# The middle stage's attention: probabilities turned unnormalised, four output products scaled by VectorE

## The reference

```python
q = rope(rmsnorm(x @ Wq.T, q_norm_w))        # 32 heads of 128
k, v = x @ Wk.T, x @ Wv.T                    # 8 heads of 128
# keys and values: 512 rows of a paged cache (gathered by a block table), then the 128 new ones
scores = q @ keys.T / sqrt(128) + mask       # 640 keys for each query
probs  = softmax(scores)                     # rows sum to 1
ctx    = probs @ values
out    = ctx.reshape(128, 32 * 128) @ Wo.T   # a sum over the 32 heads
```

## Time and profile before

| | |
|---|---|
| time, median of 3 runs | 1362.9 us (1361.45 to 1364.13) |
| span of the profiled execution | 1360.4 us |
| busy TensorE (matmul) | 1317.0 us, 97% |
| busy VectorE | 1077.3 us, 79% |
| busy ScalarE | 862.2 us, 63% |
| busy GpSimd | 653.2 us, 48% |

### The profile page before, as it was taken

One profiled execution on the slowest core, in us unless ns is written; L12 is line 12 of the kernel. 1 busy time (PEld: TensorE's weight loads), 2 busy tenths in 40 slices (PEclk: granted clock), 3 DMA queues, 4 the chain that ended last, 5 costly groups with the idle time before them and its releaser, 6 DMA issues.

```text
span 1360.4 us, 26524 instructions
## 1 busy us (share of the span) xinstructions
PE 1317.0 (97%) x8104; PEld 1132.6 (83%) x8104; DVE 1077.3 (79%) x2964; ACT 862.2 (63%) x2501; POOL 653.2 (48%) x647
## 2 busy tenths in 40 slices
PE   6899997899999999999999999999999999999998
PEld 4666765688888888888888888888888888888878
DVE  4689777688878887888888888888878888888876
ACT  2677777566766666667666766666666666666651
POOL 0455466443644464436543654465345534554531
PEclk8899998999999999999999999999999999999999
DMA  8444544544121212131223122222212121212121
GB/s 285 149 157 153 158 155 137 151 125 109 32 63 32 79 32 63 34 81 35 55 44 81 35 54 49 68 48 47 65 45 63 32 79 32 63 32 67 34 78 63
DMA packets 196400, 107.59 MB, mean 79 GB/s; under 512 B 140961, under 2 KB 180898, under 8 KB 195106
## 3 DMA queue, kind: packets, MB, share of 16 engines
q1 hardware_dynamic: 195248, 105.71, 28.9%
q10 hardware_dynamic: 1010, 0.17, 0.1%
HBM read 101.66 MB, written 37.75 MB: 102 GB/s over the span
## 4 chain that ended last, share of the span: by engine, by line
PE 90%; DVE 4%; ACT 2%; issue 1%; POOL 1%; DMA 0%; SPq 0%; DVEq 0%; ACTq 0%; POOLq 0%
PE ps L1221 12%; PE ps L1223 12%; PE ps L1222 12%; PE ps L1272 10%; PE ps L1293 5%; PE ps L1286 5%; PE ps L1287 5%; PE ps L1306 4%; PE ps L1312 4%; PE ps L1305 4%; PE ps L247 2%; PE ps L1248 2%; PE ps L259 2%; PE ps L306 1%; PE ps L297 1%
## 5 line engine op out<-in xcount | busy, mean ns | idle before, releaser
L1427 ACT ACTIVATE b_pf<-b_sm,b_nb,b_rstd 128x640 f32<-128x640 f32 x256 | 235.1, 918 | 101.8 <-DVE b_nb L1536 101.7
L1433 ACT ACTIVATE b_p_h<-ps 128x640 fp32r<-128x640 f32 x256 | 180.5, 705 | 180.3 <-PE ps L1272 179.8
L1550 DVE TENSOR_TENSOR b_p_l<-ps,b_p_h 128x640 fp32r<-128x640 f32 x256 | 210.6, 823 | 80.6 <-ACT b_p_h L1433 73.1
L1529 DVE CUSTOM_DVE_ANT_0 b_sm<-ps,mask_row 128x640 f32<-128x640 f32 x256 | 209.0, 816 | 1.4 <-issue 0.4
L1272 PE MATMUL ps<-ident,b_pf 128*128 128x128 f32 x1280 | 181.7, 273 | 4.6 <-DVE b_p_l L1550 3.0
L1545 DVE TENSOR_SCALAR b_pf<-b_pf,b_ri 128x640 f32<-128x640 f32 x256 | 159.4, 623 | 28.1 <-DVE b_ri L1542 0.9
L1221 PE MATMUL ps<-b_w_h,x1t_h 128*128 128x512 f32 (+1 forms) x512 | 179.3, 350 | 0.3 <-DVE b_w_l L1611 0.3
L1221 PE MATMUL ps<-b_kt_h,b_qt_h 128*128 128x320 f32 x512 | 173.7, 339 | 1.5 <-DVE b_mx L1529 1.4
L1222 PE MATMUL ps<-b_w_l,x1t_h 128*128 128x512 f32 (+1 forms) x512 | 173.4, 339 | 0.0
L1223 PE MATMUL ps<-b_w_h,x1t_l 128*128 128x512 f32 (+1 forms) x512 | 172.8, 338 | 0.0
L1272 PEld LDWEIGHTS ps<-ident,b_pf 128*128 128x128 f32 x1280 | 151.9, 140 | 24.7 <-issue 5.3
(11 more groups left out here) (170 smaller groups left out, 3233.1 us busy)
## 6 DMA issues: line engine op xcount, KB each, us to landing
kv_of_batch<-in_kv SPq DMA_DIRECT2D x128, 256.0 KB
b_ck<-kv_of_batch SPq DMA_DIRECT2D x64, 256.0 KB, 3.7
b_cv<-kv_of_batch SPq DMA_DIRECT2D x256, 64.0 KB, 2.2
raw<-in_w SPq DMA_DIRECT2D x32, 384.0 KB, 5.2
raw<-in_wo SPq DMA_DIRECT2D x32, 256.0 KB, 3.8
a_xt<-in_xt SPq DMA_DIRECT2D x8, 256.0 KB, 5.5
a_xin<-in_x SPq DMA_DIRECT2D x8, 256.0 KB, 5.4
x<-a_x SPq DMA_DIRECT2D x8, 256.0 KB, 5.3
```

What stands on the lines that cost most here:

```text
L1427: act.activation(pf[:, h % 2], sm[:, h % 2], ACT.Exp, bias=nb[:, m.b % 2, h:h + 1], scale=rstd[:, m.b % 4, h:h + 1], accum_out=rs[:, m.b % ...
L1433: act.activation(p_h[:, :, h * P:(h + 1) * P], turned_row, ACT.Copy).then_inc(ph_sb, 1)
L1529: dve.tensor_tensor_reduce(sm[:, h % 2], score_row, mask_row[:, m.b], 1.0, MASKED, ALU.add, ALU.max, mx[:, k, h:h + 1]).then_inc(mx_sb, 1)
L1550: dve.tensor_tensor(p_l[:, :, cols], turned_row, p_h[:, :, cols], ALU.subtract).then_inc(pl_sb, 1)
```

## The change

The probabilities are turned as the exponential left them. The reciprocal of the row sums is taken once for each item, for four heads. The output product is made for one head at a time, in three matmuls, and each head's product has a bank to itself until VectorE has multiplied it with the head's reciprocal and added it to `hacc`. There are two banks for it, `SM` for heads 0 and 3, and `OT` for heads 1 and 2 (`OT` is free once the values have been split). The semaphore `h_sb` now counts heads, not items.

```diff
+        OUT = (SM, OT, OT, SM)
             def turn_probs(m, h):
-                pe.wait_ge(pn_sb, REP * m.n + h + 1)
+                pe.wait_ge(exp_sb, REP * m.n + h + 1)
...
             def values_of_highs(m):
-                wait(pe, ol_sb, m.n)
+                wait(pe, h_sb, REP * m.n - 1)
...
-            def out_of_highs(m):
...
-            def out_of_lows(m):
...
+            def out(m, h):
+                if h == 0:
+                    if m.n == 0:
+                        pe.wait_ge(xl_sb, B)
+                    pe.wait_ge(ol_sb, m.n + 1)
+                    pe.wait_ge(wol_sb, KT * (m.g + 1))
+                    wait(pe, h_sb, REP * m.n)
+                if h == 2:
+                    pe.wait_ge(h_sb, REP * m.n + 2)
+                tile = slice(h * P, (h + 1) * P)
+                three(ps[:, OUT[h], :], (o_h[:, tile], o_l[:, tile]), (wo_h[:, h], wo_l[:, h])).then_inc(wo_ps, 1)
...
@@ TensorE, slot @@
                 if last:
-                    out_of_highs(last)
+                    out(last, 0)
+                    out(last, 1)
                 if m:
                     turn_probs(m, 2)
                 if one:
                     scores(one, 0)
                 if last:
-                    out_of_lows(last)
+                    out(last, 2)
+                    out(last, 3)
...
@@ ScalarE, exponent @@
+                if h == 0:
+                    wait(act, ri_sb, m.n - 1)
...
@@ VectorE @@
-            def invert(m, h):
-                dve.wait_ge(exp_sb, REP * m.n + h + 1)
-                k = m.b % 2
-                dve.reciprocal(ri[:, k, h:h + 1], rs[:, k, h:h + 1]).then_inc(ri_sb, 1)
-                dve.wait_ge(ri_sb, REP * m.n + h + 1)
-                hold(dve)
-                dve.tensor_scalar(pf[:, h % 2], pf[:, h % 2], ri[:, k, h:h + 1], None, ALU.mult).then_inc(pn_sb, 1)
+            def invert(m):
+                dve.wait_ge(exp_sb, REP * (m.n + 1))
+                dve.reciprocal(ri[:, m.b % 2], rs[:, m.b % 2]).then_inc(ri_sb, 1)
...
-            def accumulate(m):
...
+            def accumulate(m, h):
+                dve.wait_ge(wo_ps, REP * m.n + h + 1)
+                if h == 0:
+                    dve.wait_ge(ri_sb, m.n + 1)
+                wait(dve, h_sb, REP * m.n + h)
+                hold(dve)
+                share = ri[:, m.b % 2, h:h + 1]
+                if m.g == 0 and h == 0:
+                    dve.tensor_scalar(hacc[:, m.b], ps[:, OUT[h], :], share, None, ALU.mult).then_inc(h_sb, 1)
                     return
+                dve.scalar_tensor_tensor(out=hacc[:, m.b], in0=ps[:, OUT[h], :], scalar=share, in1=hacc[:, m.b],
+                                         op0=ALU.mult, op1=ALU.add).then_inc(h_sb, 1)
...
@@ VectorE, slot @@
                     maxima(m, 3)
                     bias(m, 3)
+                if last:
+                    accumulate(last, 0)
+                    accumulate(last, 1)
                 if two:
                     rope_products(two)
...
                     low(m, 2)
-                    invert(m, 3)
                 if one:
                     maxima(one, 0)
                 if last:
-                    accumulate(last)
+                    accumulate(last, 2)
+                    accumulate(last, 3)
```

More of the change, by code:

```diff
@@ L872, in phase3 @@
 def phase3(nc, ctx, t, ident, w_h, w_l, x1t_l, cw, sw, raw, hacc, x1_dram, out, ps, x1_out,
-           k_ps, qab_sb, kab_sb, wql_sb, wkvl_sb, qtl_sb, knl_sb, mx_sb, pl_sb, ol_sb, h_sb):
+           k_ps, qab_sb, kab_sb, wql_sb, wkvl_sb, qtl_sb, knl_sb, mx_sb, pl_sb, h_sb):
     sb = lambda n, s, d=F32: ctx.enter_context(nc.sbuf_tensor("c_" + n, s, d))
@@ L942, in turn @@
             pe.wait_ge(qtl_sb, DONE)
-        pe.wait_ge(h_sb, DONE - B + b + 1)
+        pe.wait_ge(h_sb, REP * (DONE - B + b + 1))
         for i in range(KT):
@@ L964, in gate @@
         if b == 2:
-            pe.wait_ge(ol_sb, DONE)
-            pe.wait_ge(h_sb, DONE)
+            pe.wait_ge(h_sb, REP * DONE)
         wait(pe, y_sb, b - 2)
@@ L1130, in phase2 @@
         knh_sb, knl_sb, vch_sb, vcl_sb = sem("knh_sb"), sem("knl_sb"), sem("vch_sb"), sem("vcl_sb")
-        mx_sb, nb_sb, exp_sb, ri_sb, pn_sb = sem("mx_sb"), sem("nb_sb"), sem("exp_sb"), sem("ri_sb"), sem("pn_sb")
+        mx_sb, nb_sb, exp_sb, ri_sb = sem("mx_sb"), sem("nb_sb"), sem("exp_sb"), sem("ri_sb")
         ph_sb, pl_sb = sem("ph_sb"), sem("pl_sb")
@@ L1161, in phase2 @@
             nc, ctx, t, ident, w_h, w_l, x1t_l, cw, sw, raw, hacc, x1_dram, out, ps, x1_out,
-            k_ps, qab_sb, kab_sb, wql_sb, wkvl_sb, qtl_sb, knl_sb, mx_sb, pl_sb, ol_sb, h_sb)
+            k_ps, qab_sb, kab_sb, wql_sb, wkvl_sb, qtl_sb, knl_sb, mx_sb, pl_sb, h_sb)
         block = ctx.enter_context(nc.Block())
@@ L1364, in _ @@
             low_rows(pe, 0)
-            out_of_highs(end)
-            out_of_lows(end)
+            for h in range(REP):
+                out(end, h)
             batches(pe)
@@ L1386, in out_weights @@
                 act.wait_ge(raw_in[c], 16 * (2 * g + 2))
-                wait(act, wo_ps, B * g)
+                wait(act, wo_ps, REP * B * g)
                 act.activation(wo_h[:, c], raw[:, c, 0:D], ACT.Copy).then_inc(woh_sb, 1)
@@ L1436, in output @@
                 act.wait_ge(pv_ps, m.n + 1)
-                wait(act, wo_ps, m.n)
+                wait(act, wo_ps, REP * m.n)
                 act.activation(o_h[:], ps[:, OT, :], ACT.Copy).then_inc(oh_sb, 1)
@@ L1554, in output @@
                 dve.tensor_tensor(o_l[:], ps[:, OT, :], o_h[:], ALU.subtract).then_inc(ol_sb, 1)
-            def accumulate(m):
-                dve.wait_ge(wo_ps, m.n + 1)
-                if m.g == 0:
-                    dve.tensor_copy(hacc[:, m.b], ps[:, SM, :]).then_inc(h_sb, 1)
+            def accumulate(m, h):
[7 more added lines that the diff above has]
+                    dve.tensor_scalar(hacc[:, m.b], ps[:, OUT[h], :], share, None, ALU.mult).then_inc(h_sb, 1)
                     return
-                dve.tensor_tensor(hacc[:, m.b], ps[:, SM, :], hacc[:, m.b], ALU.add).then_inc(h_sb, 1)
+                dve.scalar_tensor_tensor(out=hacc[:, m.b], in0=ps[:, OUT[h], :], scalar=share, in1=hacc[:, m.b],
+                                         op0=ALU.mult, op1=ALU.add).then_inc(h_sb, 1)
             h_rest, choose, rows_dve = dve_ffn
@@ L1573, in slot @@
                 if m:
-                    invert(m, 0)
                     bias(m, 1)
@@ L1579, in slot @@
                     queries(one)
+                if last:
+                    invert(last)
                 if m:
-                    invert(m, 1)
                     maxima(m, 2)
@@ L1584, in slot @@
                     low(m, 0)
-                if m:
-                    invert(m, 2)
                 if last:
@@ L1623, in _ @@
             h_rest(dve, 2)
+            invert(end)
             output(end)
-            accumulate(end)
+            for h in range(REP):
+                accumulate(end, h)
             rows_dve(dve)
```

## The result

The changed kernel takes 1422.8 us (median of 4 runs, 1421.1 to 1423.2) against 1362.6 (4 runs, 1361.4 to 1364.1) for the kernel before on the same chip: ratio 1.0445, 95% interval 1.0432 to 1.0457. That is 60.2 us slower. Forecast were 51.5 us slower, 1414.4, with a range of 1400 to 1428.

The account below looks back on a forecast made before the run. TensorE, never idle in the middle stage's 16.73 us slots, was taken as the bound. Terms 47.1 + 3.9 + 1.5 + 2.0 - 3.0 = 51.5 us, on 1360.4 plus 2.5, gave 1414.4 us, range 1400 to 1428.

Parts of the forecast that it names:

- regular wait: TensorE before head 2's output product, waiting for head 1's accumulation on VectorE: 0.76 us in each of 62 slots, 47.1 us.
- The start at 3.45: Head 0's accumulation on VectorE starts 3.45 us after the turn of head 1, where the rotary product stood.
- The handover of 0.15: From VectorE's end to the waiting TensorE matmul's start: 0.15 us, ends 0.05 and 0.25.
- The seven long biases: Seven slots where head 3's bias beside GpSimd's weight split takes 0.71 instead of 0.16 us: 3.9 us added.
- last slot: No next item's scores cover the accumulations there: wait 1.5 us instead of 0.76.
- end: After the last slot, four products and accumulations one after the other delay the last stage by 2.0 us.
- gains: TensorE waits before turns, behind scalings held beside GpSimd, partly go: 3.0 us saved, ends 0 and 6.
- VectorE's busy time: Over the whole kernel, down by some 58 us: 190 of scalings and reciprocals gone, 132 of accumulations more.
- What is late next: After the wait, GpSimd's rotary sum and head 2's residual still fit, by 0.8 and 0.7 us.
- Rival 1 (hidden): Relieved VectorE finishes head 1's accumulation early enough, so no wait before head 2's product: 1362 us, chance 0.08.
- Rival 2 (slow accumulation): VectorE's accumulations take 0.9 to 1.1 us each, lengthening the wait by 0.4 to 0.8 us: 1440 to 1465, chance 0.07.
- Rival 3 (the clock): A pause in each slot lowers TensorE's granted clock, to a mean of 0.93: about 1495 us, chance 0.02.

Follow-up runs that it names:

- e8: Changed kernel with the rotary products ahead of the accumulations of heads 0 and 1: 1505.5 us, ratio 1.1049.
- e1: Changed kernel with the k and v projection ahead of the output products of heads 2 and 3: 1379.0 us, ratio 1.0129.
- e7: Changed kernel with banks SM, OT, SM, OT, projection ahead of heads 2 and 3, rotary products between accumulations of heads 0 and 1: 1380.7 us, ratio 1.0139.
- e9: e7 with the banks the other way round (OT, SM, OT, SM): 1364.2 us, ratio 1.0011.
- e6: Kernel before the change with the k and v projection ahead of its four low output matmuls: 1361.3 us, ratio 0.9992.
- e4: Changed kernel with constant 1.0 instead of the reciprocal as accumulation factor, no-operation kept: 1412.9 us in its profiled run, 7447.4 in the other, no ratio.
- e5: e4 also without the no-operation ahead of the accumulation: 1409.8 us, ratio 1.0347.
- e3: Kernel before the change with the division by the row sum left out, turns waiting for the exponential: 1360.0 us, ratio 0.9986.
- e2: Changed kernel with only the banks alternating (SM, OT, SM, OT): 1394.2 us, ratio 1.0232.

## Why the prediction was right, and where it was off

Of the 9.2 us between the forecast's 51.5 and the 60.7 of the two spans, the regular wait makes 13.0, and the terms below the rest: -3.9, +0.3, +0.4, +1.6 and -2.2.

- **The mechanism and its place: shown.** One wait per slot, before head 2's product, for the accumulation of head 1. Making it longer costs in full (e8), taking it away gives the time back (e1, e7, e9), and moving blocks without it does nothing (e6).
- **The regular wait is the mis-sized term:** forecast 0.76 us, measured 0.97, times 62 a difference of 13 us. The pieces, as the forecast had them: TensorE is there at 4.35, forecast 4.33. The start at 3.45 was 3.56: 0.07 of it is the no-operation ahead of the accumulation (e4 against e5), 0.04 is open. I had taken the place of the rotary product, which has none. "0.69 us" each was 0.75: the factor per row (e4), a piece that my nearest rows, L1561 and L812 in the earlier trace rows, did not have. The distance between the two, 0.11, was 0.10. The handover of 0.15 from the earlier trace rows was 0.06; those rows hold an accumulator read, whose result perhaps comes later than its row ends. Missing altogether was the restart, 0.10 us for the first matmul after a wait. Together 0.11 + 0.12 - 0.01 - 0.09 + 0.10 - 0.02 = 0.21, as measured.
- **The seven long biases: wrong, 0 instead of 3.9 us.** The bias beside GpSimd's split, 0.71 us in the earlier trace rows, is 0.26 now and the accumulation behind it starts at 3.56 as elsewhere. GpSimd beside it, in the kernel before and after, and VectorE after:

```profile
628.62 2.40 POOL L1640 TENSOR_TENSOR b_w_l<-raw,b_w_h 128x1024 fp32r<-128x1024 f32 x1
```

```profile
646.26 2.40 POOL L1643 TENSOR_TENSOR b_w_l<-raw,b_w_h 128x1024 fp32r<-128x1024 f32 x1
```

```profile
648.41 0.26 DVE L1534 SCALAR_TENSOR_TENSOR b_nb<-b_mx,b_rstd 128x1 f32<-128x1 f32 x1
648.62 1.60 DVE L1560 SCALAR_TENSOR_TENSOR b_hacc<-ps,b_ri,b_hacc 128x512 f32<-128x512 f32 x2
```

In both traces, and in all seven slots, the bias ends within 0.02 us of the end of GpSimd's instruction (before 630.32 + 0.71 = 631.03 and 628.62 + 2.40 = 631.02, after 648.67 and 648.66). How long it is held so depends on how late it starts beside that instruction, and in the longer slot it starts later. The step took a duration from the trace of before as a property of the instruction, when it was one of what GpSimd did beside it at that moment. In e1, where the slot is nearly as long as before, the seven biases take 0.68 to 0.73 us again. That this term came out as nothing was luck: it hid 3.9 us of the mis-sized wait.
- **The small terms:** last slot 1.8 (forecast 1.5), end 2.4 (2.0), gains 5.2 (3.0, with ends of 0 and 6). The 1.6 us behind a late transfer were in no term. That VectorE's relief is worth next to nothing, e3 shows: 2.3 us.
- **The range** has a slip: two thirds of the way from 0.76 down to 0.58 is 0.64 and not 0.62, half of the way up to 1.21 is 0.98 and not 0.95. The measured time lies inside either way.
- **VectorE's busy time** fell by 43 us and not by 58: some 250 accumulations of 0.06 us more are 15.
- **What is late next:** the residual of head 2 had 0.7 us of room in the forecast and was not late in the changed kernel. But this room was the wait itself: where TensorE no longer stood (e1), the residual was late by 0.1.
- **Rival 1 (hidden)** needed the second accumulation to end 4.18 us after the turn of head 1; it ends at 5.16. **Rival 2 (slow accumulation)** needed 0.9 us; 0.75 is a small step toward it. The rule of the Trainium skill, Vector Engine (DVE) Microarchitecture Reference, "Points that are easy to get wrong", would halve the rate of this instruction with two SBUF sources that are not bf16; with one of them in PSUM no row here shows anything like it (690 ns with a constant factor, as for a plain addition).
- **Rival 3 (the clock)**: in the changed kernel the granted clock is 1.00 in 600 to 900 us, the 2.4 GHz level, with TensorE pausing 0.7 us by the profile in every slot, and it stays there through the whole middle stage. The Trainium skill, TensorE: Matmul & The Clock Gate, "A second HAM failure mode: psum-queue depth-cycling", tells of clock changes under pauses between groups of matmuls; the trace disagrees for pauses of this length. For longer ones it agrees: in e8, with 1.8 us by the profile in every slot, the clock fell six times, and in e3 once, behind a pause of 4.4 us. The rival did not come true here, but a wait twice as long brings it about, at some 1.7 us for each fall.

## What to carry to other kernels

Ask of every result that gets a bank of its own who must have emptied that bank before, and put work of the waiting engine between: here the same instructions cost 60 us in one order and 1.5 us in another. On a saturated engine count for each wait also its restart, and find short waits by the distance of the starts, not by the idle time in the view. An instruction's price is taken from a row with the same kinds of operands and the same predecessor, and a duration that shows contention holds only for the moment it was read in. And look at the granted clock of every run whose waits grew: a time can meet its expectation for the wrong reason (e8).

## What the hardware did that I had not expected

- A 128x512 matmul that had to wait lasts 0.50 instead of 0.39 us, and the next starts 0.33 instead of 0.23 behind it: each wait costs 0.10 us on top (the changed kernel, e2, e7, e8). The length alone does not prove a wait: behind the five transposes of a turn the first 128x512 product lasts 0.48 us in the kernel before too, with no idle time in the view.
- A factor per row, read from SBUF, costs VectorE 0.06 us per 128x512 instruction against a constant: 750 and 690 ns.
- A no-operation ahead of VectorE's instruction costs 0.07 us behind a one-column instruction (e5) and nothing that shows behind a 128x512 one (e8, where it starts 0.08 before that one's end).
- VectorE's dependent accumulations lie 0.85 us apart, 0.10 after the end of the first; two independent rotary products start 0.60 apart, 0.08 before the end of the first. The dependence through `hacc` so costs 0.18 us.
- Pauses of 0.9 us every 17.7 us leave TensorE's granted clock at 1.00 in all slots. Pauses of 2.0 us every 18.8 us (e8, by the issue) take it to 0.50 six times, for 3.4 us each, 20 to 660 us apart.
- A 128x1 `scalar_tensor_tensor` with both inputs in SBUF that meets GpSimd's 128x1024 subtraction ends with it: 0.16 us alone, 0.71 to 1.00 in the kernel before, 0.26 to 0.28 in the changed one.
